# A gated cross-attention kernel: gate's rows parted at 512 instead of 416, the last tile in one PE step and three pieces, and a last chunk of 32 rows

## The reference

```
memory_proj = einsum('bme,de->bmd', memory, W_mem)
scores = einsum('bnd,bmd->bnm', hidden_states, memory_proj) / sqrt(D)
memory_context = einsum('bnm,bmd->bnd', softmax(scores), memory_proj)
gate_input = concatenate([hidden_states, memory_context], axis=-1)
gate = sigmoid(einsum('bnf,df->bnd', gate_input, W_gate) + b_gate)
fused = hidden_states + gate * memory_context
out = fused * rsqrt(mean(square(fused), axis=-1) + 1e-6) * norm_w
```

## Time and profile before

| | us |
|---|---|
| median of 3 runs (299.37 to 299.94) | 299.92 |
| profiled execution | 300.07 |
| its span, from first to last instruction | 298.3 |
| PE busy | 292.5 (98%) |
| DVE busy | 164.1 (55%) |
| ACT busy | 156.4 (52%) |
| mean granted clock of TensorE, of full speed | 0.996 |

### The profile page before, as it was taken

How to read it: one execution, slowest core, us unless ns; L and a number is a source line. 1 busy time by engine, 2 the same in 40 slices (tenths; PEclk the granted TensorE clock), 3 DMA queues, 4 the chain that set the end, 5 groups by cost and what they waited for, 6 DMA issues and landing times.

```text
span 298.3 us, 4078 instructions
## 1 busy us (share of the span) xinstructions
PE 292.5 (98%) x1674; PEld 281.3 (94%) x1674; DVE 164.1 (55%) x232; ACT 156.4 (52%) x227; POOL 3.0 (1%) x9
## 2 busy tenths in 40 slices
PE   8999999999999999999999999999999999999993
PEld 8999999898999989899898989999999999999993
DVE  3657454557575565855557553423457662543663
ACT  5547345454573736548363525543467773643563
POOL 0000000000000000000000000000000000010001
PEclk9999999999999999999999999999999999999998
DMA  6998391644729467383944020177223400000235
GB/s 207 406 369 268 105 357 34 229 132 135 243 99 313 149 210 247 98 265 116 288 182 145 20 70 8 64 286 294 74 70 142 141 2 1 0 2 8 109 114 211
DMA packets 18450, 46.34 MB, mean 155 GB/s; under 512 B 1520, under 2 KB 3312, under 8 KB 18432
## 3 DMA queue, kind: packets, MB, share of 16 engines
q1 hardware_dynamic: 18432, 46.09, 45.2%
HBM read 42.80 MB, written 3.28 MB: 154 GB/s over the span
## 4 chain that ended last, share of the span: by engine, by line
PE 98%; DVE 0%; issue 0%; DVEq 0%
PE ps L290 69%; PE ps L408 11%; PE ps L384 11%; PE ps L398 1%; PE ps L304 1%; PE ps L415 1%; PE ps L488 1%; PE ps L315 0%; PE ps L318 0%; PE ps L476 0%; DVE x_again L911 0%; PE ps L325 0%; PE ps L330 0%; PE ps L321 0%; PE ps L327 0%; PE ps L468 0%
## 5 line engine op out<-in xcount | busy, mean ns | idle before, releaser
L290 PE MATMUL ps<-act_hi,w_hi 128*128 128x400 f32 (+4 forms) x272 | 79.5, 342 | 0.0
L290 PE MATMUL ps<-act_hi,w_lo 128*128 128x400 f32 (+4 forms) x272 | 78.9, 340 | 0.0
L290 PE MATMUL ps<-act_lo,w_hi 128*128 128x400 f32 (+4 forms) x272 | 78.8, 340 | 0.0
L290 PEld LDWEIGHTS ps<-act_hi,w_hi 128*128 128x128 f32 x272 | 49.9, 188 | 0.9
L290 PEld LDWEIGHTS ps<-act_lo,w_hi 128*128 128x128 f32 x272 | 50.6, 188 | 0.1
L290 PEld LDWEIGHTS ps<-act_hi,w_lo 128*128 128x128 f32 x272 | 50.6, 188 | 0.0
L711 DVE TENSOR_TENSOR w_lo<-w_stage,w_hi 128x1024 fp32r<-128x1024 f32 (+2 forms) x23 | 26.0, 1131 | 24.3 <-ACT w_hi L523 23.2
L711 DVE TENSOR_TENSOR cn_lo<-cn_stage,cn_hi 128x1536 fp32r<-128x1536 f32 (+2 forms) x24 | 28.6, 1217 | 6.4 <-ACT cn_hi L542 5.6
L711 DVE TENSOR_TENSOR ct_lo<-ct_stage,ct_hi 128x1444 fp32r<-128x1444 f32 x16 | 25.8, 1654 | 0.5 <-ACT ct_hi L534 0.5
L523 ACT ACTIVATE w_hi<-w_stage 128x1024 fp32r<-128x1024 f32 x20 | 21.0, 1054 | 6.7 <-PE ps L290 4.9
L607 ACT ACTIVATE pc<-ps,row_inv 100x512 f32<-100x512 f32 x8 | 5.5, 687 | 34.3 <-PE ps L408 34.3
(11 more groups left out here) (105 smaller groups left out, 446.2 us busy)
## 6 DMA issues: line engine op xcount, KB each, us to landing
ct_stage<-ctxT SPq DMA_DIRECT2D x16, 722.0 KB, 9.8
cn_stage<-ctxN SPq DMA_DIRECT2D x8, 768.0 KB, 5.8
cn_stage<-ctxN SPq DMA_DIRECT2D x8, 512.0 KB
w_stage<-w_gate_x SPq DMA_DIRECT2D x8, 512.0 KB, 8.9
w_stage<-w_gate_mc SPq DMA_DIRECT2D x8, 512.0 KB, 3.6
x_again<-xT SPq DMA_DIRECT2D x1, 3200.0 KB, 11.3
acc<-xT SPq DMA_DIRECT2D x6, 400.0 KB, 7.9
w_stage<-w_mem_t SPq DMA_DIRECT2D x4, 512.0 KB, 5.6
```

What stands on the lines that cost most here:

```text
L290: done = nc.tensor.matmul(o, wgt, stream[h][part], start=first and wgt is wh and part == 0, stop=last and wgt is wl, skip_group_check=onto)
```

## The change

- FIRST becomes 512: eight steps of 512 columns and eight of 288. Tile 7's second range is one step on PE, so there are 16 steps instead of 17, and the mean and inverse of the first rows are over four times 128 instead of four times 104.
- The last 288 rows leave in chunks of 128, 128 and 32 rows. For the last step ACT and DVE work in three pieces of these widths: three sigmoids, then for each piece product and sum on DVE, and square and weighing on ACT.
- Each chunk's mean is two matmuls now (`chunk_mean`): the sums of tiles 0 to 6 and the square of tile 7. PE turns tiles 0 to 6 of chunks 0 and 1 ahead (14 tiles), then for each the mean and its last tile.
- For the 32 rows ACT's weighing also writes them into `small`, four feature tiles side by side (4 x 32 rows), so two transposes turn the eight tiles. The squares' sums are copied four times over, so that each of the 128 partitions has its row's mean. The chunk then lies as partition (u, row), 256 features, and its store, of 128 KB, is 128 pieces of 1 KB.
- The stores of the first rows grow from 416 KB to 512 KB each.

```diff
-FIRST, CHUNK = 416, 128
-ROWS2, LATE = (R - FIRST) // CHUNK, R - CHUNK
+FIRST, SMALL = 512, 32
+CHUNKS = ((FIRST, FIRST + P), (FIRST + P, FIRST + 2 * P), (R - SMALL, R))
+PAIRS = P // SMALL
+NC = len(CHUNKS)
-    + [(t, FIRST, R) for t in range(1, KD - 1)] + [(KD - 1, FIRST, LATE), (KD - 1, LATE, R)]
+    + [(t, FIRST, R) for t in range(1, KD)]
@@ sync
-            for i in range(ROWS2):
+            for i in range(NC):
                 sp.wait_ge(row_left, i + 1)
                 sp.wait_ge(row_right, i + 1)
+                if i < NC - 1:
+                    sp.dma_start(out_rows[i * P:(i + 1) * P, :],
+                                 row_out[:, i * D:(i + 1) * D]).then_inc(stored, 16)
+                else:
+                    sp.dma_start(out_rows[i * P:i * P + SMALL, :].rearrange("r (u c) -> u r c", u=PAIRS),
+                                 row_out[:, i * D:i * D + D // PAIRS]).then_inc(stored, 16)
@@ tensor
+            def chunk_mean(i):
+                a, b = CHUNKS[i]
+                sums, last = (square_sum[:, a:b], square[:, LAST % 2, a - FIRST:b - FIRST]) if i < NC - 1 \
+                    else (small_sum[:, 0, :], small_sum[:, 1, :])
+                pe.wait_ge(squared, LAST + 1 + i)
+                nc.tensor.matmul(late_mean(i), sums, mean_w[:, :], start=True, stop=False)
+                nc.tensor.matmul(late_mean(i), last, mean_w[:, :], start=False, stop=True).then_inc(late_mean_made, 1)
+            def turn_small():
+                for j in range(2):
+                    done = nc.tensor.transpose(bank(TURN[NC - 1][j], P), small[:, j, :], ident[:, :])
+                return done
-            pe.wait_ge(summed, LAST)
-            for i in range(ROWS2 - 1):
-                done = nc.tensor.matmul(late_mean(i), late_sums(i), mean_w[:, :], start=True, stop=True)
-            done.then_inc(late_mean_made, 1)
             pe.wait_ge(weighted, LAST)
-            turn(0, 0, KD).then_inc(turned, 1)
...
+            turn(0, 0, KD - 1)
             pe.wait_ge(out_done, KD)
-            turn(1, 0, KD).then_inc(turned, 1)
-            pe.wait_ge(weighted, LAST + 1)
-            turn(2, 0, KD).then_inc(turned, 1)
+            turn(1, 0, KD - 1)
+            pe.wait_ge(summed, LAST + 1)
+            for i in range(NC - 1):
+                chunk_mean(i)
+                pe.wait_ge(weighted, LAST + 1 + i)
+                turn(i, KD - 1, KD).then_inc(turned, 1)
+            chunk_mean(NC - 1)
+            pe.wait_ge(weighted, LAST + NC)
+            pe.wait_ge(mean_copied, 2)
+            turn_small().then_inc(turned, 1)
@@ scalar, in weigh
+                if r1 == R:
+                    nc.scalar.activation(small_part(t), acc[:, t, R - SMALL:R], ACT.Copy, scale=norm_t[:, t:t + 1])
+                    r1 = R - SMALL
@@ scalar, the last step
+            for a, b in CHUNKS:
+                at = slice(a - FIRST, b - FIRST)
+                nc.scalar.activation(gate[:, LAST % 2, at], gate_bank(LAST)[:, at], ACT.Sigmoid,
+                                     bias=bias_t[:, KD - 1:KD]).then_inc(gate_done, 1)
...
+            for i, (a, b) in enumerate(CHUNKS):
+                part = acc[:, KD - 1, a:b]
+                act.wait_ge(fused, LAST + 1 + i)
+                if i < NC - 1:
+                    nc.scalar.activation(square[:, LAST % 2, a - FIRST:b - FIRST], part,
+                                         ACT.Square).then_inc(squared, 1)
+                else:
+                    nc.scalar.activation(small_sum[:, 1, :].rearrange("p (u r) -> p u r", u=PAIRS),
+                                         part.unsqueeze(1).to_broadcast([P, PAIRS, SMALL]),
+                                         ACT.Square).then_inc(squared, 1)
+                act.wait_ge(squared, LAST + 1 + i)
+                nc.scalar.activation(part if i < NC - 1 else small_part(KD - 1), part, ACT.Copy,
+                                     scale=norm_t[:, KD - 1:KD]).then_inc(weighted, 1)
@@ vector, after sum_squares(LAST - 1)
+            dve.wait_ge(summed, LAST)
+            nc.vector.tensor_copy(small_sum[:, 0, :].rearrange("p (u r) -> p u r", u=PAIRS),
+                                  square_sum[:, R - SMALL:R].unsqueeze(1).to_broadcast([P, PAIRS, SMALL]))\
+                .then_inc(summed, 1)
+            for i, (a, b) in enumerate(CHUNKS):
+                part = gate[:, LAST % 2, a - FIRST:b - FIRST]
+                dve.wait_ge(gate_done, LAST + 1 + i)
+                nc.vector.tensor_tensor(part, part, mc[:, KD - 1, a:b], ALU.mult).then_inc(gated, 1)
+                dve.wait_ge(gated, LAST + 1 + i)
+                nc.vector.tensor_tensor(acc[:, KD - 1, a:b], part, x_again[:, KD - 1, a:b],
+                                        ALU.add).then_inc(fused, 1)
...
+            late_mean_plus_eps(0)
+            late_mean_plus_eps(1)
+            right_half(0)
+            late_mean_plus_eps(2)
+            right_half(1)
+            right_half(2)
```

More of the change, by code:

```diff
@@ L96, in build @@
         rms = sb(top, "rms", [FC, 4])
-        rms_late = sb(top, "rms_late", [CHUNK, ROWS2])
+        rms_late = sb(top, "rms_late", [P, NC])
+        small = sb(top, "small", [P, 2, P])
+        small_sum = sb(top, "small_sum", [P, 2, P])
         rms_diag = sb(top, "rms_diag", [FC, 4, FC])
@@ L120, in build, with late_mean, small_part @@
         G2B, RIB = 4, 3
-        def late_mean(i, n=1):
-            return bank(6, n, CHUNK, 8 + i) if i < ROWS2 - 1 else bank(7, n, CHUNK, BANK - 1)
+        def late_mean(i):
+            return bank(MEANS[i], 1, P, 8)
+        def small_part(t):
+            return small[:, t % 2, t // 2 * SMALL:(t // 2 + 1) * SMALL]
         def gate_bank(n):
@@ L687, in _ @@
             act.wait_ge(gx_saved, 2 * B)
-            for n in range(LAST + 1):
+            for n in range(LAST):
                 if n in SPLIT_AT:
                     split_gate_w(SPLIT_AT[n])
-                early = n == END0 + 1 or n >= LAST - 1
+                early = n == END0 + 1
                 if early:
@@ L698, in _ @@
                     finish(n - 1)
[L699 to L702, removed]
+            finish(LAST - 1)
+            act.wait_ge(gate_made, LAST + 1)
+            act.wait_ge(fused, LAST - 1)
+            for a, b in CHUNKS:
+                at = slice(a - FIRST, b - FIRST)
+                nc.scalar.activation(gate[:, LAST % 2, at], gate_bank(LAST)[:, at], ACT.Sigmoid,
+                                     bias=bias_t[:, KD - 1:KD]).then_inc(gate_done, 1)
+            act.wait_ge(summed, LAST - 1)
+            for i, (a, b) in enumerate(CHUNKS):
[11 more added lines that the diff above has]
+                                     scale=norm_t[:, KD - 1:KD]).then_inc(weighted, 1)
+            for i in range(NC):
+                act.wait_ge(late_rooted, i + 1)
                 act.wait_ge(turned, i + 1)
-                nc.scalar.activation(row_out[:, i * D:i * D + BANK], bank(TURN[i][0], BANK, CHUNK), ACT.Copy,
+                turned_left = bank(TURN[i][0], BANK if i < NC - 1 else P)
+                nc.scalar.activation(row_out[:, i * D:i * D + turned_left.shape[1]], turned_left, ACT.Copy,
                                      scale=rms_late[:, i:i + 1]).then_inc(row_left, 1)
@@ L908, in right_half, with late_mean_plus_eps @@
+            def late_mean_plus_eps(i):
+                dve.wait_ge(late_mean_made, i + 1)
+                nc.vector.tensor_scalar(rms_late[:, i:i + 1], late_mean(i), EPS, None, ALU.add).then_inc(mean_copied, 1)
             def right_half(i):
-                dve.wait_ge(late_rooted, 1 + (i == ROWS2 - 1))
+                dve.wait_ge(late_rooted, i + 1)
                 dve.wait_ge(turned, i + 1)
-                nc.vector.tensor_scalar(row_out[:, i * D + BANK:(i + 1) * D], bank(TURN[i][1], BANK, CHUNK),
+                turned_right = bank(TURN[i][1], BANK if i < NC - 1 else P)
+                cols = turned_right.shape[1]
+                nc.vector.tensor_scalar(row_out[:, i * D + cols:i * D + 2 * cols], turned_right,
@@ L929, in _ @@
             nc.gpsimd.tensor_tensor(rms[:, :], rms[:, :], minus_half[0:FC, :], ALU.pow).then_inc(rooted, 1)
[L930 to L933, removed]
+            for i in range(NC):
+                pool.wait_ge(mean_copied, i + 2)
+                part = rms_late[:, i:i + 1]
+                nc.gpsimd.tensor_tensor(part, part, minus_half[:, 0:1], ALU.pow).then_inc(late_rooted, 1)
 def kernel(x, ctx_1024, L0_xattn_W_mem, L0_xattn_W_gate, L0_xattn_b_gate, L0_xattn_norm_w):
```

36 lines of the change are left out of this document (7 added, 29 removed).

## The result

The change makes the kernel slower: 301.63 us in the median (301.23 to 301.74, 6 runs) against 299.80, a ratio of 1.0062 with a 95% interval of 1.0049 to 1.0075, some 1.8 us. 299.4 was forecast, with 300.2 as the upper end. The profiled execution took 301.65 us, its span is 299.7, against 300.07 and 298.3 before.

A forecast was written before the change was run, and what follows sets the result against it. Bound by PE's matmul-to-matmul pace up to the last gate step, then by what follows it. Gate steps -1.7, mean and inverse +0.1, first row store +0.97, bytes +0.05: -0.6 us against 300.07, forecast 299.4, range 298.3 to 300.2.

The forecast's parts named there:

- What bounds the kernel, and the end as first issue plus bytes: PE's matmul pace to the last gate step; then end is first row store's issue plus 0.83, bytes, 0.96 us.
- Part 1: Gate steps on PE: 71.2 us become 69.5, a gain of 1.7 us (1.1 to 2.1).
- Part 2: ACT and DVE work fits the shorter 3.18 us second steps, costing nothing; first rows' mean and inverse +0.1 us.
- Part 3: From T, PE's last gate record's end, to the first row store: T+4.05 against T+3.08, +0.97 us (0.6 to 1.5).
- Part 4: Final row stores' bytes: the 128 KB third piece goes over four transfer engines, +0.05 us against the 512 KB one before.
- (a): Last small store spread over sixteen engines, ending 0.96 us or slightly more sooner: -1.6, 298.4 us; chance 0.25.
- (b): Last small store on two engines or at half rate from 1 KB runs: 2.7 us, total 300.7 to 300.9; chance 0.05.
- (c): DVE and ACT chain before the first row store longer, issue at T+4.6: -0.05, 300.0 us; chance 0.12.
- (d): In the gate steps, fewer matmuls bring nothing, the 288 step held at a floor; about 300.5 us; chance 0.03.
- The sum: Whole kernel: -1.7+0.1+0.97+0.05 = -0.6 us against 300.07, forecast 299.4 among runs.

The follow-up runs named there:

- (row, pair): Changed kernel with the small chunk's partitions ordered row first, pair innermost, outermost count 128 on both sides of its store: 299.75 us, ratio 0.9986; again 299.30 us, 0.9989.

## Why the prediction was wrong, point by point

- **What bounds the kernel, and the end as first issue plus bytes.** Right. With the one (row, pair) store and with three plain stores of 128 rows the end follows from the first row store's issue and the bytes (T+8.66 and T+9.55, worked out as T+8.6 and T+9.5). It does not where SP's issues come late (four stores, T+9.28) or the pace is not 410 GB/s (96 rows, T+9.7).
- **Part 1, the gate steps.** The mechanism was right, the size wrong, below the range given (0.7 us where 1.1 to 2.1 was said). The term mis-sized is the 512 step: 229.5 ns was taken from the attention's matmuls, and from carrying 416 on by 1/2.4 ns a column. But the excess over N/2.4 grows with the width, and measured were 233 ns, 44.7 us for the eight steps instead of 44.1. The attention's matmuls load 100 columns of weights and the gate's 128; whether that makes the difference was not tried. The 288 steps took 25.7 us instead of 25.4; interpolation between 256 and 384 was good. The 66.3 us that the prediction drew from the Trainium skill, "TensorE: Matmul & The Clock Gate", section "Back-to-back issue gap", do not follow from that formula: by N/2.4 plus 2.5 ns alone the steps before come to 65.0, and no gain; 66.3 takes the 128 column step at its measured 109 ns. The section also gives the formula for an isolated matmul, not for a stream of loads and matmuls as here.
- **Part 2.** Right: the outputs end at T, and ACT and DVE never held PE up. Mean and inverse cost 0.16 instead of 0.1.
- **Part 3, the first row store at T+4.05.** Right, T+3.94, and link by link: the epsilon was forecast at T+2.28 and came at T+2.27.
- **Part 4, the bytes.** The step that failed and decided the sign. The count of engines was right: the share of 0.28 at 98 GB/s is four of sixteen. The Trainium skill, "DMA: Bandwidth & Descriptors", section "Why a DMA increments its semaphore by 16 and not by 1", states just that count for an outermost dimension of 4, and the trace agrees, as it does with sixteen for counts of 32 and 128. But "1.3 us for 128 KB" took the pace for the price. With 1.1 us ahead of the pace and an uneven end (31 GB/s from 298.7 on, in windows of 0.1 us) it was 2.79 us. The row it was read from, the 82-row piece of the earlier trace rows, shows a pace in the midst of the bytes, nine microseconds after the issue, and not a start. The 1.3 us is the mis-sized term, and it had no allowance for a slow start.
- **Rivals.** (a) did not come by itself, but is the (row, pair) form, where its arithmetic held: 0.3 us for the small store by the ends (T+8.66 against T+8.35 without it). (b) named the place and nearly the price (2.7 us against 2.79), but by the wrong mechanism: two engines would show a share near 0.13 all along, and the 1 KB runs are the same in the (row, pair) form. That the price fits is luck. It had a chance of 0.05, and the range stopped at 300.2 and so left it out; its time, 300.7 to 300.9, is 0.7 to 0.9 short, since it counted on the full gain of the gate steps. (c) did not come. (d) was wrong in its reason: at 133 to 134 ns the 288 step is clear of the floor of 111; what ate the gain of the parting is the 512 step.
- **The sum.** Forecast -0.6, measured +1.6 between the two profiled executions: of the 2.2 us between, 1.0 come from the gate steps and 1.5 from the last store; the rest is small and goes to both sides.

## What to carry to other kernels

Look at the outermost count of both sides of a store at the end of a kernel: behind other stores the same 128 KB moved the end by 0.3 us with a count of 128 and by 2.5 us with a count of 4 (T+8.66 and T+10.88 against T+8.35 without the store), and only the order of the partitions differed. Price a short last transfer by a row of the same shape in the same place. A row from the midst of its bytes shows a pace and no start, and even the store by itself, 1.75 us from first byte to last, would have priced too low the 2.79 that it took behind another. A narrower step on one side of a parting is paid for by a wider one on the other: add up the pair, from measured widths, before crediting a new parting.

## What the runs showed of the hardware that I had not expected

- A store carried by four engines comes late to its pace: about 1.1 us of 4 to 16 GB/s behind another store, about 0.5 us by itself, whether it writes 1 KB or 33 KB apart in HBM. By itself the share is 0.14 to 0.30 in that time; behind another store single pieces of 1 KB alternate with empty windows. The cause is open.
- SP needs 0.66 to 0.67 us to issue a small store with a view of three dimensions, behind others or by itself, and 0.33 to 0.35 us to issue one of 128 rows of 4 KB. One of 128 runs of 1 KB took 0.33 by itself and 0.51 behind others, and four of 32 partitions in a row took 0.51, 1.15, 0.42 and 0.42.
- A store of 96 partitions moves at 262 to 279 GB/s at a full share, one of 128 at 400.
- The pace over N/2.4 ns is no constant: a floor of 111 ns up to 224 columns, 11 ns over at 256, 15.5 at 384 to 416, 18 to 21 at 512.
